# Graph attention with LayerNorm on one core: three bias or residual adds made by GpSimd's adding DMAs, a reworked prologue and another ScalarE order

## The reference, cut to what matters

```python
h = jnp.einsum('bnd,ade->bane', feat_in, W)
th = jnp.tanh(h)
attn_src = jnp.einsum('bane,aeo->bano', th, w_src)
attn_dst = jnp.einsum('bane,aeo->bano', th, w_dst)
attn = attn_src + jnp.swapaxes(attn_dst, 2, 3)
attn = jnp.where(attn >= 0, attn, LEAKY_ALPHA * attn)
attn = jnp.where(mask, jnp.float32(-999.0), attn)
attn = jax.nn.softmax(attn, axis=-1)
feat_out = jnp.einsum('banm,bame->bane', attn, h) + b
feat_out = jax.nn.elu(feat_out)                    # heads side by side
gate = jax.nn.sigmoid(feat_in @ H_w.T + H_b)
return gate * feat_out + (1.0 - gate) * feat_in    # then layernorm(x + this)
```

## Time and profile before

| what | value |
|---|---|
| median of 3 runs | 749.0 us (747.43 to 750.62) |
| the profiled execution's own time | 748.52 us |
| its span in the trace | 746.7 us |
| PE, DVE, POOL, ACT busy | 92%, 93%, 80%, 51% of the span |

### The profile page before, as it was taken

One profiled execution on the slowest core, in us unless ns is written; L12 is line 12 of the kernel. 1 busy time (PEld: TensorE's weight loads), 2 busy tenths in 40 slices (PEclk: granted clock), 3 DMA queues, 4 the chain that ended last, 5 costly groups with the idle time before them and its releaser, 6 DMA issues.

```text
span 746.7 us, 12632 instructions
## 1 busy us (share of the span) xinstructions
PE 684.6 (92%) x3411; PEld 395.1 (53%) x3472; DVE 691.3 (93%) x1281; ACT 377.5 (51%) x804; POOL 596.5 (80%) x437
## 2 busy tenths in 40 slices
PE   4399999999999999999999999999999999999970
PEld 4355555555565555656555565655646465563430
DVE  8779999999999999999999999999999999999876
ACT  5123537374564637456473746547274654727161
POOL 6884697998979798897979889797988989793500
PEclk9599999999999999999999999999999999999995
DMA  5300111113121111212111121211211131111102
GB/s 184 99 1 2 57 43 43 58 43 100 44 98 42 45 58 47 89 42 98 42 55 60 51 73 42 98 42 69 64 49 57 42 98 42 57 43 43 42 2 84
DMA packets 32875, 43.82 MB, mean 59 GB/s; under 512 B 1234, under 2 KB 26580, under 8 KB 32852
## 3 DMA queue, kind: packets, MB, share of 16 engines
q1 hardware_dynamic: 24660, 31.35, 13.5%
q10 hardware_dynamic: 8192, 12.19, 4.5%
HBM read 30.95 MB, written 12.58 MB: 58 GB/s over the span
## 4 chain that ended last, share of the span: by engine, by line
PE 72%; DVE 17%; issue 5%; ACT 3%; DMA 2%; DVEq 1%; SPq 0%; POOL 0%; ACTq 0%; POOLq 0%
PE out_T L826 37%; PE hg L750 24%; DVE ew L610 9%; PE tr L834 5%; PE vb L812 4%; DVE ex L645 2%; PE hg L797 1%; DVE sd L559 1%; DMA ew<-in_HwT 1%; DVE th_w L541 1%; ACT x_plus L415 1%; PE hg L802 1%; DVE att L628 1%; ACT h_sb L381 1%; DVE ex L704 1%
## 5 line engine op out<-in xcount | busy, mean ns | idle before, releaser
L610 DVE SCALAR_TENSOR_TENSOR ew<-vb,u,adj_in 128x512 f32<-128x512 f32 x768 | 533.0, 737 | 2.3 <-PE vb L812 2.3
L826 PE MATMUL out_T<-ew,vals 128*64 128x512 f32 x1536 | 360.0, 600 | 3.3 <-DVE ew L610 1.3
L826 PEld LDWEIGHTS out_T<-ew,vals 128*64 128x64 f32 x1536 | 110.0, 136 | 194.5 <-issue 161.3
L258 POOL TENSOR_TENSOR th_w<-th,score_w 128x768 f32<-128x768 f32 x60 | 110.1, 1835 | 67.2 <-ACT th L380 61.6
L410 ACT ACTIVATE att_T<-out_T,tiny 128x512 f32<-128x512 f32 x96 | 66.1, 688 | 163.2 <-PE out_T L826 163.1
L750 PE MATMUL hg<-w_hi,xT_hi 128*128 128x384 f32 x384 | 109.7, 394 | 19.3 <-ACT xT_hi L371 7.7
L750 PE MATMUL hg<-w_hi,xT_lo 128*128 128x384 f32 x384 | 88.6, 338 | 0.3 <-DVE xT_lo L526 0.3
L750 PE MATMUL hg<-w_lo,xT_hi 128*128 128x384 f32 x384 | 88.2, 337 | 0.0
L750 PEld LDWEIGHTS hg<-w_hi,xT_hi 128*128 128x128 f32 x384 | 70.3, 194 | 27.2 <-issue 23.3
L262 POOL TENSOR_TENSOR th_w<-th_w 128x384 f32<-128x384 f32 x60 | 80.2, 1337 | 4.7
L387 ACT ACTIVATE gate_tanh<-hg 128x384 f32<-128x384 f32 x64 | 31.4, 490 | 95.7 <-PE hg L750 95.7
(11 more groups left out here) (97 smaller groups left out, 759.6 us busy)
## 6 DMA issues: line engine op xcount, KB each, us to landing
xT_in<-in_xT SPq DMA_DIRECT2D x16, 768.0 KB, 4.6
x_in<-in_x SPq DMA_DIRECT2D x16, 768.0 KB, 4.5
out<-y ACTq DMA_DIRECT2D x15, 768.0 KB, 3.5
adj_in<-in_adjT SPq DMA_DIRECT2D x16, 256.0 KB, 4.8
ew<-in_W SPq DMA_DIRECT2D x1, 576.0 KB, 4.2
ew<-in_HwT SPq DMA_DIRECT2D x1, 576.0 KB, 8.1
score_w<-in_w_rows SPq DMA_DIRECT2D x1, 384.0 KB, 7.1
out<-y SPq DMA_DIRECT2D x1, 384.0 KB, 2.5
```

Of the source, the lines that this page charges most:

```text
L258: g.tensor_tensor(th_w[:, c % 2], th[:, c].unsqueeze(1).broadcast_to([P, 2, D]), score_w[:], ALU.mult).then_inc(S["thw_done"], 1)
L610: ve.scalar_tensor_tensor(out=ew[:, (2 * C * j + i) % SLOTS, :], in0=VB[h % 4][:], scalar=u[:, q, c, h:h + 1], in1=adj_in[:, q, c, :], op0 ...
L826: te.matmul(OUT[VW * k:VW * k + VW, :], vals[:, q, c, h, :], ew[:, t % SLOTS, :], start=(c == 0), stop=(c == C - 1)).then_inc(S["ew_free"], 1)
```

## The change

Three additions leave the engines and become DMAs that add their source to what lies in SBUF (`accum_op=ALU.add`), all issued by GpSimd: the bias on `h_sb` (was L272), the gate bias on `gate_tanh` (was the tenth matmul of each gate), and x on the gated difference `y` (was L302). The gates are copied unchanged out of PSUM and the tanh is taken once over all four chunks after the gate bias has been added. The features are copied with the 1 added. Biases come from the host laid out as one row of 1536, which each partition reads.

ScalarE's `x_forms` moves behind features chunk 1 and `normalise`. In the prologue the gate weights move behind the scores (ScalarE) and into step 0 (VectorE), GpSimd no longer adds or splits beside VectorE's score sums, TensorE runs idle matmuls (`warm_up`) into `tr0`, `head_sel` is made in two stages, and VectorE weights the tanh of chunks 0 and 1 of graph 1.

```diff
@@ GpSimd
             def add_bias(b):
-                pool.wait_ge(S["hcopy_done"], C * b + C)
-                g.tensor_tensor(h_sb[:].rearrange("p c (h e) -> p (c h) e", e=E), h_sb[:].rearrange("p c (h e) -> p (c h) e", e=E),
-                                bias_row[:].unsqueeze(1).broadcast_to([P, C * H, E]), ALU.add).then_inc(S["hb_done"], 1)
+                pool.dma_start(h_sb[:].rearrange("p c d -> p (c d)"), bias_rows, accum_op=ALU.add).then_inc(S["add_bias"], 16)
+
+            def add_gate_bias(b):
+                pool.dma_start(gate_tanh[:].rearrange("p c d -> p (c d)"), gate_bias_rows,
+                               accum_op=ALU.add).then_inc(S["add_gate_bias"], 16)

-            def add_rows(b, q):
-                pool.wait_ge(S["hb_done"], b + 1)
+            def add_rows(b, q, first=True):
+                if not first:
+                    pool.wait_ge(S["mixed"], 2 * (b - 2) + 4)
+                pool.wait_ge(S["add_bias"], 16 * b + 16)
                 g.tensor_tensor(hb_sum[:], h_sb[:, 0:2], h_sb[:, 2:4], ALU.add).then_inc(S["hb_sum_done"], 1)
+                if not first:
+                    add_x(b - 2)
                 pool.wait_ge(S["hb_sum_done"], 2 * b + 1)
...
-                g.tensor_tensor(ex[:], gate[:], ex[:], ALU.mult).then_inc(S["mixed"], 1)
-                pool.wait_ge(S["mixed"], 3 * b + 5)
                 pool.wait_ge(S["st_y"], 16 * b + 16)
-                g.tensor_tensor(y[:], x_in[:], ex[:], ALU.add).then_inc(S["mixed"], 1)
+                g.tensor_tensor(y[:], gate[:], ex[:], ALU.mult).then_inc(S["mixed"], 1)
+
+            def add_x(b):
+                pool.dma_start(y[:], x_v[b], accum_op=ALU.add).then_inc(S["add_x"], 16)
...
@@ GpSimd, step
+                if not last:
+                    add_bias(b + 1)
                 if not first:
                     subtract_x(b - 1)
                     mix(b - 1)
-                if not last:
-                    add_bias(b + 1)
-                    add_rows(b + 1, 1 - q)
+                if last:
+                    pool.wait_ge(S["mixed"], 2 * (b - 1) + 4)
+                    add_x(b - 1)
+                if not last:
+                    add_rows(b + 1, 1 - q, first)
                     values(b + 1, 1 - q)
...
+                add_gate_bias(b)
@@ GpSimd, prologue
+                pool.wait_ge(S["scores"], 1)
+                pool.wait_ge(S["hcopy_done"], C)
                 add_bias(0)
-                for c in range(C):
+                for c in range(2):
                     split_low(1, 1, c)
                 pool.wait_ge(S["dve_setup"], DVE_SETUP)
                 values(0, 0)
                 add_rows(0, 0)
+                for c in range(2, C):
+                    split_low(1, 1, c)
@@ ScalarE
-                a.activation(gate_tanh[:, c], G_BANK[c][:, 0:D], ACT.Tanh, scale=0.5).then_inc(S["gate_done"], 1)
+                a.activation(gate_tanh[:, c], G_BANK[c][:, 0:D], ACT.Copy).then_inc(S["gate_done"], 1)
...
             def gate_quarter(b):
-                act.wait_ge(S["gate_done"], C * b + C)
-                act.wait_ge(S["mixed"], 3 * b + 2)
+                act.wait_ge(S["add_gate_bias"], 16 * b + 16)
+                a.activation(gate_tanh[:], gate_tanh[:], ACT.Tanh, scale=0.5).then_inc(S["tanh_done"], 1)
+                act.wait_ge(S["tanh_done"], b + 1)
+                act.wait_ge(S["mixed"], 2 * b + 2)
...
             def row_sums(b):
-                act.wait_ge(S["mixed"], 3 * b + 6)
+                act.wait_ge(S["add_x"], 16 * b + 16)
@@ ScalarE, features
                 a.activation(th[:, c], feature_bank(b, c)[:, 0:D], ACT.Tanh).then_inc(S["th_done"], 1)
+                if isinstance(b, int) and b == 1:
+                    act.wait_ge(S["vals_done"], c + 1)
+                    act.wait_ge(S["hb_sum_done"], 1)
@@ SP
                     sp.wait_ge(S["x_forms_done"], b)
-                    sp.wait_ge(S["mixed"], 3 * b + 3)
                 sp.dma_start(x_in[:], x_v[b]).then_inc(S["ld_x"], 16)
@@ TensorE
-                products(G_BANK[c], q, c, D, [(gate_bias_sel[:], gate_bias[:])]).then_inc(S["g_done"], 1)
+                products(G_BANK[c], q, c, D, [], waits).then_inc(S["g_done"], 1)
...
+            def warm_up(n, l, r):
+
+                for _ in range(n):
+                    te.matmul(TR[:, 0:r.shape[1]], l, r, start=True, stop=True)
```

More of the change, by code:

```diff
@@ L31, in gat_layernorm @@
     B, N, D = x.shape
-    E = bias.shape[0]
+    E = bias.shape[1]
     H = D // E
@@ L38, in gat_layernorm @@
     SLOTS = 16
-    SETUP = 19
-    DVE_SETUP = 12
+    SETUP = 17
+    DVE_SETUP = 7
+    WARM = 12
     NPART = 3
@@ L322, in step @@
                 if not last:
-                    for c in range(C):
+                    for c in range(2 if first else 0, C):
                         weigh(b + 1, c)
+                if not last:
+                    add_bias(b + 1)
                 if not first:
@@ L333, in step @@
                     mean(b - 1)
-                if ahead:
-                    for c in range(C):
-                        split_low(b + 2, q, c)
+                if not ahead:
+                    pool.wait_ge(S["gate_done"], C * b + C)
+                for c in range(C if ahead else 0):
+                    if c == 0:
+                        pool.wait_ge(S["gate_done"], C * b + C)
+                    split_low(b + 2, q, c)
+                add_gate_bias(b)
                 if not first:
@@ L364, in before @@
                 copy_vT(0, 0)
+                act.wait_ge(S["ld_wg"], 16)
+                a.activation(w_hi[:, :, D:2 * D], w_gate_in, ACT.Copy).then_inc(S["w_hi_done"], 1)
             def split(b, q, c):
@@ L374, in features @@
                 act.wait_ge(S["h_done"], C * b + c + 1)
-                act.wait_ge(S["vals_done"], C * b)
-                if isinstance(b, int) and b == 1:
-                    act.wait_ge(S["hb_sum_done"], 1)
+                if not isinstance(b, int) or b > 1:
+                    act.wait_ge(S["vals_done"], C * b)
                 if not isinstance(b, int) or b:
@@ L448, in step @@
             def step(b, q, first, last, ahead=True):
-                if not first:
-                    x_forms(b - 1)
                 if not last:
@@ L456, in step @@
                     features(b + 1, 1)
+                if not first:
+                    x_forms(b - 1)
                 copy_out(b, 0)
@@ L667, in step @@
                         between[8] = [lambda: head_sums(b + 1, 1)]
+                    if j == 1 and first:
+                        between[2] = [lambda: head_products(1, 0)] + between[2] + [gate_low]
+                        between[8] = [lambda: head_products(1, 1)] + between[8]
                     if j == 1 and not first:
@@ L722, in before @@
                 te.sem_inc(S["ew_free"], SLOTS)
+                pe.wait_ge(S["dve_setup"], 3)
+                warm_up(WARM, v_parts[:, 0], v_parts[:].rearrange("p c n -> p (c n)"))
                 pe.wait_ge(S["w_hi_done"], 1)
@@ L762, in features @@
                 pe.wait_ge(S["xlo_done"], C * b + c + 1)
-                if c == 0:
+                if isinstance(b, int) and b == 1:
+                    if c == 0:
+                        pe.wait_ge(S["vT_done"], b)
+                    elif c > 1:
+                        pe.wait_ge(S["hcopy_done"], C + c - 1)
+                elif c == 0:
                     pe.wait_ge(S["vT_done"], b)
@@ L785, in gates @@
             def gates(b, q, c, last):
+                waits = {}
+                if isinstance(b, int) and b == 0 and c == 0:
+                    pe.wait_ge(S["w_hi_done"], 2)
+                    waits = {KD: (S["w_lo_done"], 2)}
                 if c > 1:
@@ L817, in attend @@
                     pe.wait_ge(S["outT_copied"], HP * b + j)
-                if j == 0:
+                if j == 0 and (not isinstance(b, int) or b):
                     pe.wait_ge(S["vals_done"], C * b + C)
                 for c in range(C):
+                    if j == 0 and isinstance(b, int) and b == 0:
+                        pe.wait_ge(S["vals_done"], c + 1)
                     for k in range(2):
```

110 lines of the change are left out of this document (56 added, 54 removed).

## The result

| what | value |
|---|---|
| median of the kernel changed, 4 runs | 785.6 us (783.72 to 788.49) |
| median of the kernel before, 4 runs beside them | 748.34 us (747.43 to 750.62) |
| ratio, with its 95% interval | 1.0497 [1.0467, 1.0527] |
| the profiled execution's own time, and its span | 788.49 us, 786.8 us |

The change made the kernel 5.0% slower, where 736 us was forecast. The page of the kernel changed: busy time by engine, and the granted clock in 40 slices, as in the earlier trace rows.

A forecast was written before the change was run, and what follows sets the result against it. TensorE and VectorE were taken to share the bound. Prologue -6.0, loop -7.5 (15 steps of 1.0 gained less 0.5 for x's late landing) and end +0.9 gave -12.6, from 748.5 to 736 us; range 723 to 762.

The forecast's parts named there:

- the landing of x on y: Loop: the DMA adding x lands 0.7 us late for ScalarE's row sums, 0.5 beyond the slack, each step.
- The flight: Loop: x's adding DMA takes 6.0 us from issue to landing, the middle of 3.5 and 8.0.
- The issue: Loop, GpSimd: issuing a DMA takes 0.5 us of the engine, between 0.4 and 3.5.
- The slot: Loop, ScalarE: row sums of y start at 325.50, with GpSimd's mixing beginning at 310.66.
- the slower rival: Loop: a flight of 8.0 lands y 2.7 us late, 2.5 beyond slack; 766 us in all, chance 0.22.
- The rule that spoke for the change: GpSimd-issued DMA: about 2.0 us plus bytes at 436 GB/s, 3.8 for x; y in time, sum 7.5 us better.
- The loop's gains: Loop, TensorE: 1.0 us a step from shorter gates and an earlier tanh, before 0.5 lost to x's late landing.
- the tenth matmul: Loop, TensorE: each gate loses one matmul, worth 0.18 us a gate, 0.7 us a step for four.
- x + 1: Loop, ScalarE: moving this pass later starts the features' tanh, and so TensorE, 0.3 us earlier a step.
- GpSimd's time: Loop: GpSimd sheds two passes of 3.5 us; the 7 us are worth nothing by themselves, being off the chain.
- The prologue: Start to first `alone`: 6.0 us saved, between 3 and 8, with that `alone` near 37.4 against 43.88.
- The end: After the loop: last gates save 0.7 us, the extra tanh adds 1.6, net +0.9.

The follow-up runs named there:

- feature_bias_on_engine: The changed kernel with x and the features' bias added by GpSimd's own passes again, only the gate bias still an adding DMA: 735.8 us.
- idle_matmuls_in_gap: The changed kernel with ten useless matmuls filling TensorE's stall before the transposes of pair 4: 773.41 us, ratio 1.034 to the kernel before.

## Why the prediction was wrong

**The step that failed** is the landing of x on y, put at 0.7 us late with 0.2 of slack. The mechanism was named in full, its slower case too, and the signs written down for it came: landings over 7 us, an issue over 1 us, a VectorE wait for the transposes over 1.3. What failed is the size of the lateness, of which three inputs were off, all to the same side:

- *The flight*, 6.0 us taken as the middle of 3.5 and 8.0. It was 7.2 to 7.5: 1.2 to 1.5 too short. The range of flights up to 7.7 held it.
- *The issue*, 0.5 us "nearest to the other issues", measured 0.93 for the bias and 1.33 for x, and the pass beside the bias's issue took 3.77 instead of 3.48. x was issued 10.0 us after the bias's issue began, not 9.5: 0.5 more. (Where no bias is issued beside it, in feature_bias_on_engine, that pass took 3.49.)
- *The slot.* The prediction kept the row sums 14.84 us behind the start of the mixing (325.50 - 310.66). Gate 3 is now out 14.3 us behind the bias's issue (338.43 - 324.13), 0.5 less. Two of the shortened gates lie between, which would account for 0.4 of it; their gain had been counted on one side of the sum alone.
- Together 0.7 + 1.2 + 0.5 + 0.5 = 2.9 us, the wait in the rows above.

**Not in the sum at all** was TensorE's clock. Stalls of 2.8 to 3.4 us inside an engine that is else busy were followed by 1.2 GHz in nine steps, and idle_matmuls_in_gap prices this at 16.8 us. The parts add up to 748.5 - 5.4 - 10.5 + 38.4 + 0.9 = 771.9 us without the clock, and to 788.7 with it, against 788.5 in the profile. (They are differences of the same traces, so that they meet is book-keeping and not a test.) So the range, which ended at 762, failed on the lateness alone: 2.9 us a step beyond the slack, where 762 allowed 2.2 and the slower rival 2.5. The clock then added 16.8 us, which no rival had, and the time came out some 20 us above the slower rival's 766.

**The rule that spoke for the change.** The row shows 7.5 us for x's adding DMA of 768 KB. The estimate of 3.8 us by the Trainium skill, "DMA: Bandwidth & Descriptors", section Anatomy of one DMA, disagrees by half. The plain copies from GpSimd, 4.2 and 5.0 us, come nearer to it. An add needs two source reads by the Trainium skill, "Collectives: The Full Stack", section The bandwidth ceiling: the fold count and why AG ≠ RS ≠ AR. With the bytes counted twice the estimate was 5.6 us, which is nearer. The direction agrees (adding costs 2.2 to 2.4 us over the plain copy), the size is still short.

**The loop's gains**, predicted 1.0 us a step, were 0.70 over all 15 (646.9 - 636.4 = 10.5) and 0.76 over steps 1 to 13: the tenth matmul 0.66 for 0.7, x + 1 0.22 for 0.3. The first was read nearly right, of the second the step keeps less. Together they are 0.9, so 0.1 us a step is lost elsewhere in the change, and where is not shown. That VectorE has room for them and does not cap them was right: it is busy 41.26 of 42.46 us.

**GpSimd's time**, "worth nothing", was worth 0.36 us a step where the features' bias is concerned. It is still true that nobody on the chain waits for it; what the saying missed is that VectorE's pass over `ex` took 2.39 instead of 2.06 us when GpSimd's passes beside it came at other times.

**The prologue**, 6.0 predicted, gave 5.4. Its inner steps came nearly as written: weightings at 0.96 from 11.57 on, the maxima at 19.84 for 19.5, the first edge at 24.93 for 25.5. From there to `alone` 13.5 us passed instead of 11.9, as the weighting and the low part took 2.02 and 2.12 beside GpSimd's values and sums, instead of 0.96 and 1.36. The table load behind a wait was overlooked, but cost under 1 us at `alone`. **The end**, +0.9, came out as +0.9, and not by luck: with the tenth matmul back it is 57.4 us instead of 56.7, so the shorter gates are worth the 0.7 predicted, and the added tanh took 1.47 us for 1.6.

## What to carry to other kernels

An add taken from an engine and given to a DMA is paid in latency: before doing it, place the landing (issue, flight and the reader's new slot, all in one time line) against the reader, and move the reader behind independent work if it is within a few us. Then look for what moved along with the reader: here the gate bias's DMA stood behind the mean, and its later landing cost 4 us at the end. A late landing on an engine in front of TensorE's input cost its own length less the slack, and a second amount where TensorE's clock fell after the gap. When a change combines several edits and comes out slower, put them back one at a time: here one edit hid a gain of 2% from the others.
